# Four banks for the weight products, key products one step sooner, and a new order of the small layers

## The reference

```python
x = x + L0_xattn(layernorm(x), ctx, mask, ...)
x = x + L0_ffn(layernorm(x), ...)
x = x + L1_xattn(layernorm(x), ctx, Wq, bq, Wk, bk)
x = x + L1_ffn(layernorm(x), qweight, ...)
```

## Time and profile before

| | |
|---|---|
| median of 3 runs | 986.61 us (985.14 to 986.87) |
| the profiled execution's own time | 985.75 us |
| its span | 983.9 us |
| TensorE busy | 954.6 us, 97% of the span |
| VectorE busy | 603.1 us, 61% |
| ScalarE busy | 395.0 us, 40% |
| GpSimd busy | 470.3 us, 48% |

### The profile page before, as it was taken

The page is one execution under the profiler, slowest core; times in us unless marked ns, Lnnn a source line. Parts: engine busy times, 40 slices in busy tenths (PEclk is TensorE's granted clock), DMA queues, the critical chain, the costliest instruction groups (busy, mean ns, idle before and its releaser), DMA issues.

```text
span 983.9 us, 16715 instructions
## 1 busy us (share of the span) xinstructions
PE 954.6 (97%) x5645; PEld 835.4 (85%) x5645; DVE 603.1 (61%) x1123; ACT 395.0 (40%) x1101; POOL 470.3 (48%) x528
## 2 busy tenths in 40 slices
PE   8999999999999999999999999999999997998995
PEld 7888888888898888888888888888888886776774
DVE  5674773656566566666565656565656577274874
ACT  5655443343434343433333333334343432324553
POOL 2450735464545545555555464555554511022577
PEclk9999999999999999999999999999999999899999
DMA  9233536747474656565555656464747442111001
GB/s 335 88 95 125 171 137 210 261 157 276 156 273 161 257 176 238 190 220 190 217 200 209 219 191 241 168 257 162 256 170 261 151 150 87 52 66 33 1 34 54
DMA packets 58185, 169.60 MB, mean 172 GB/s; under 512 B 5767, under 2 KB 7947, under 8 KB 57884
## 3 DMA queue, kind: packets, MB, share of 16 engines
q1 hardware_dynamic: 58140, 169.01, 48.5%
HBM read 158.51 MB, written 10.49 MB: 172 GB/s over the span
## 4 chain that ended last, share of the span: by engine, by line
PE 91%; DVE 4%; issue 2%; ACT 1%; POOL 1%; DMA 1%; SPq 0%; POOLq 0%; ACTq 0%; DVEq 0%
PE ps_q L325 6%; PE ps_q L326 6%; PE ps_q L327 6%; PE ps_v L325 6%; PE ps_v L327 6%; PE ps_v L326 6%; PE ps_o L325 6%; PE ps_o L327 6%; PE ps_o L326 6%; PE ps_t L1775 6%; PE ps_k L325 6%; PE ps_k L327 6%; PE ps_k L326 6%; PE ps_s L1748 6%; PE ps_t L1765 3%
## 5 line engine op out<-in xcount | busy, mean ns | idle before, releaser
L1203 DVE TENSOR_TENSOR acc<-ps_o,acc 128x512 f32<-128x512 f32 x128 | 87.9, 686 | 153.3 <-PE ps_o L327 153.3
L652 ACT ACTIVATE scores<-scores,neg_max 128x128 f32<-128x128 f32 x256 | 99.9, 391 | 196.3 <-DVE neg_max L1284 196.3
L325 PE MATMUL ps_v<-wv_hi,ct_hi 128*128 128x256 f32 x504 | 143.1, 284 | 1.8 <-DVE vv L1157 1.5
L327 PE MATMUL ps_v<-wv_hi,ct_lo 128*128 128x256 f32 x504 | 142.6, 283 | 0.0
L326 PE MATMUL ps_v<-wv_lo,ct_hi 128*128 128x256 f32 x504 | 142.6, 283 | 0.0
L955 POOL TENSOR_TENSOR wq_lo<-raw_q,wq_hi 128x256 fp32r<-128x256 f32 x65 | 48.2, 742 | 158.6 <-ACT wq_hi L519 158.6
L325 PE MATMUL ps_o<-wo_hi,att_hi 128*128 128x512 f32 x256 | 105.5, 412 | 0.9 <-DVE att_lo L1191 0.9
L658 ACT COPY probs_t<-ps_t 128x512 f32<-128x512 f32 x64 | 37.6, 587 | 168.1 <-PE ps_t L1765 168.1
L325 PEld LDWEIGHTS ps_v<-wv_hi,ct_hi 128*128 128x128 f32 x504 | 96.4, 191 | 6.6 <-issue 2.5
L327 PE MATMUL ps_o<-wo_hi,att_lo 128*128 128x512 f32 x256 | 100.4, 392 | 0.0
L326 PE MATMUL ps_o<-wo_lo,att_hi 128*128 128x512 f32 x256 | 100.2, 391 | 0.0
(11 more groups left out here) (335 smaller groups left out, 2396.9 us busy)
## 6 DMA issues: line engine op xcount, KB each, us to landing
ring_hi<-scratch_x_t SPq DMA_DIRECT2D x39, 512.0 KB, 4.0
ring_lo<-scratch_x_t SPq DMA_DIRECT2D x39, 512.0 KB, 5.0
ring_hi<-scratch_c_t SPq DMA_DIRECT2D x39, 512.0 KB, 4.2
ring_lo<-scratch_c_t SPq DMA_DIRECT2D x39, 512.0 KB, 5.3
raw_v<-in_w_v SPq DMA_DIRECT2D x16, 512.0 KB, 5.7
raw_o<-in_w_o SPq DMA_DIRECT2D x16, 512.0 KB, 3.3
raw_q<-in_w_q SPq DMA_DIRECT2D x15, 512.0 KB, 5.9
raw_k<-in_w_k SPq DMA_DIRECT2D x15, 512.0 KB, 5.6
```

The costliest lines, as they stand in the source:

```text
L325: pe.matmul(dst, hi_l, hi_r, start=first, stop=False)
L327: return pe.matmul(dst, lo_l, hi_r, start=False, stop=last)
L652: e = act.activation(probs[n][:, m, :], scores[n][:, m, :], ACT.Exp, bias=neg_max[:, n, m:m + 1], accum_out=row_sum[:, n, m:m + 1])
L1203: dve.tensor_tensor(acc[:, b, :], ps_o[:], acc[:, b, :], ALU.add).then_inc(o_added, 1)
```

## The change

- **Banks.** `m_banks` gives the four weight products a bank each (`ps_q`, `ps_k`, `ps_q2`, `ps_k2`); the wait on `mm_out` is gone. `product_m(1)` and `product_m(2)` stand ahead of the matrix-vector block, with transpose and values of step 62; `product_m(3)` stands behind it. Scores of step 63 and the first half of output 62 go ahead of `spread_kb`, and `product_g(0)` goes ahead of `lora_b`.
- **Key products.** `plain_k(s + 3)` stands in step `s` in place of `plain_k(s + 2)`, from step 1 on, and ScalarE's `k_evac` with it; the one at the end of step 8 goes.
- **Evacuations.** VectorE empties the value banks for steps 62 and 63 at the end of steps 60 and 61; `attention_rest(62)` moves ahead of the copy of the matrix-vector result, `mm_rest(3)` ahead of the low-rank results.
- **Context products.** One in each of the stages 0 to 3, with one quarter of the unpacking, which moves behind `b_finish` on VectorE and to the end of the stage on ScalarE.
- **Order in the stages.** `a_rest` goes ahead of the statistics of layer 2's output; from stage 8 on, `b_finish` and its statistics go ahead of `c_scale`, and GpSimd adds the shift after `inv_std(2)`. The attention of batch 7 goes to `ps_q`. `shift_rows` is made in stage 4. `c_shift_sb` has two buffers. The shift of the last tile is one VectorE operation in stage 11, in the queue ahead of `c_rest(7)`.

```diff
@@ TensorE, steps 0 to 8
             def plain_k(t, c, bank=ps_k):
                 pe.wait_ge(wk_lo_s, 2 * (t // 4) + t % 2 + 1)
-                pe.wait_ge(k_out, min(t, 4 * PLAIN - 2))
+                pe.wait_ge(k_out, t)
...
             output(0, 0, 0, (0,))
+            plain_k(4, 4)
             step_transpose(1, 1)
...
-                plain_k(s + 2, (s + 2) % LOOP_STEPS)
+                plain_k(s + 3, (s + 3) % LOOP_STEPS)
...
             plain_q(s + 3, 3, ps_q2)
-            plain_k(s + 3, 3, ps_k2)
@@ TensorE, from layer 1 to layer 3
+        m_banks = (ps_q, ps_k, ps_q2, ps_k2)
...
-                wait_from(pe, mm_out, m - 1)
...
             output(s - 1, 5, None, (0,))
             product_m(0)
             output(s - 1, 5, None, (1,))
+            product_m(1)
+            step_transpose(s, 6)
+            product_m(2)
+            step_values(s, 6)
...
-            product_m(1)
+            product_m(3)
...
+            s = STEPS - 1
+            step_scores(s, 7)
+            output(s - 1, 6, None, (0,))
             spread_kb()
-            step_transpose(s, 6)
-            product_m(2)
-            step_values(s, 6)
...
             last.then_inc(lr_mm, 1)
-            product_m(3)
-            s = STEPS - 1
-            step_scores(s, 7)
-            output(s - 1, 6, None, (0,))
+            product_g(0)
...
-            product_g(0)
             output(s - 1, 6, None, (1,))
@@ ScalarE and VectorE, from layer 1 to layer 3
             exponentials(STEPS - 2, 0)
-            mm_high(0)
-            mm_high(1)
+            pt_evac(STEPS - 2)
+            attention_high(STEPS - 2)
+            for m in range(NC):
+                mm_high(m)
             act.wait_ge(kb_mm, 1)
             act.copy(kb_row[:], ps_v[:]).then_inc(kb_s, 1)
-            pt_evac(STEPS - 2)
-            mm_high(2)
-            attention_high(STEPS - 2)
...
-            mm_high(3)
...
-                v_evac(s + 1, ((c + 1) // 2) % 2, (c + 1) % 2)
+                if not (last and c == 5):
+                    v_evac(s + 1, ((c + 1) // 2) % 2, (c + 1) % 2)
...
+                if last and c > 3:
+                    v_evac(s + 2, 1, c % 2)
...
             softmax_front(STEPS - 2, 0)
-            v_evac(STEPS - 1, 1, 1)
...
             weighted_rows(0, wq1_raw, 1)
+            attention_rest(STEPS - 2)
             dve.wait_ge(vec_mm, 1)
...
             mm_rest(2)
-            attention_rest(STEPS - 2)
+            mm_rest(3)
...
-            mm_rest(3)
             step_drain(STEPS - 1, 7)
@@ the stages, TensorE
-                wait_from(pe, b_add, b)
-                pe.matmul(ps_o[:], b_probs_t[:], ctx_sb[:, b, :], start=True, stop=True).then_inc(at_mm, 1)
+                if b < BATCH - 1:
+                    wait_from(pe, b_add, b)
+                else:
+                    pe.wait_ge(a_add, BATCH)
+                pe.matmul((ps_o, ps_q)[b // (BATCH - 1)][:], b_probs_t[:], ctx_sb[:, b, :], start=True,
+                          stop=True).then_inc(at_mm, 1)
...
-                if w < 2:
-                    product_g(4 + 2 * w)
+                if w < 4:
+                    product_g(4 + w)
...
-                if w < 2:
-                    product_g(5 + 2 * w)
@@ the stages, ScalarE
-                wait_from(act, c_rest_s, b)
-                act.mul(c_shift_sb[:], shift_rows[:], x_sum[:, b:b + 1]).then_inc(c_shift, 1)
+                wait_from(act, c_rest_s, b - 1)
+                act.mul(c_shift_sb[b % 2][:], shift_rows[:], x_sum[:, b:b + 1]).then_inc(c_shift, 1)
...
-                if w < 2:
-                    code(2 * w)
...
-                if w < 2:
-                    code(2 * w + 1)
                 if a < BATCH:
                     stage_a_zt(a)
+                if w < 4:
+                    code(w)
@@ the stages, GpSimd
-                if c >= 0:
-                    pool.wait_ge(c_shift, c + 1)
...
+                if w < BATCH and 0 <= att:
+                    shift_in(c)
                 if 0 <= att < BATCH:
                     inv_std(2, att)
+                if w >= BATCH:
+                    shift_in(c)
@@ the stages, VectorE
+                if has_a:
+                    a_rest(a)
                 if 0 <= a - 1 < BATCH:
                     statistics(1, a - 1, a_add, a)
-                if has_a:
-                    a_rest(a)
-                if w < 2:
-                    g_evac(4 + 2 * w)
-                    unpack_code(2 * w)
+                if w < 4:
+                    g_evac(4 + w)
+                if has_att and w >= BATCH:
+                    b_finish(att)
+                    statistics(2, att, b_add, att + 1)
                 if has_c:
                     c_scale(c)
...
-                if has_att:
+                if has_att and w < BATCH:
                     b_finish(att)
                     statistics(2, att, b_add, att + 1)
-                if att == 0:
+                if w < 4:
+                    unpack_code(w)
+                if w == 4:
                     dve.wait_ge(rows_in, 48)
...
+                if w == BATCH + 3:
+                    last = BATCH - 1
+                    dve.wait_ge(c_bias, BATCH)
+                    dve.wait_ge(n_xn[2], BATCH)
+                    dve.scalar_tensor_tensor(f_scr[last % 2][:], shift_rows[:], x_sum[:, last:BATCH], f_scr[last % 2][:],
+                                             ALU.mult, ALU.add).then_inc(shift_s, 1)
             dve.wait_ge(c_scaled, BATCH)
-            dve.wait_ge(c_rest_s, BATCH)
+            dve.wait_ge(shift_s, 2)
```

34 lines of the change are left out of this document (17 added, 17 removed).

## The result

| | before | with the change |
|---|---|---|
| median | 986.87 us (5 runs, 985.14 to 989.29) | 980.50 us (5 runs, 978.06 to 981.15) |
| ratio | | 0.9937, 95% interval 0.9923 to 0.9951 |
| profiled execution | 985.75 us, span 983.9 | 981.03 us, span 979.2 |

The change makes the kernel 6.4 us faster. The forecast was 976.3 us with a range up to 980.5, and the median came out at that upper end: direction right, size 10.3 us forecast and 6.4 measured. The largest part of what is missing went in the last stages, where I had a loss of 1.1 us.

What follows compares the result with a forecast made beforehand. TensorE was taken as the bound: busy throughout the loop, with waits and a lowered clock outside it. Terms -1.0 - 8.3 - 2.1 + 1.1 = -10.3 from 985.75, plus 0.86, gave 976.3 us; range 974.0 to 980.5.

Steps and rivals of the forecast that it cites:

- Key products, -1.0: Steps 1 to 8: a key product covers TensorE's 1.41 us softmax wait, less a new 0.4 us wait; lead -1.0 us.
- Transition, -8.3 with the value evacuations: Layer 1 to layer 3: weight products, transpose and values fill the 4.8 us wait before the matrix-vector products; lead -8.3 us.
- the wait of 1.3 us for the softmax: Transition: TensorE waits 1.3 us before output 62's second half, until VectorE's add behind the last softmax frees ps_o.
- both forecast waits: Transition: new TensorE waits of about 0.7 us for kb_row and 1.3 us for ps_o.
- the fall: Rival: the granted clock falls in the transition, one or two products at the lower level; 978 to 981 us, chance 0.16.
- Context products, -2.1: Layer 2's first stages, 876.8 to 924: context products over four stages end z_stack and most a_lo waits; lead -2.1 us.
- The rival that the stages gain nothing: The normalisation chain bounds each of the first four stages; 978.4 us, up to 980.5, chance 0.13.
- the new waits: Stages: TensorE waits 1.0, then some 0.4 us for the normalised tile, 0.2 to 0.35 for z_stack, 0.6 for b_full.
- The last stages, +1.1: From stage 8: VectorE's shift waits for GpSimd's bias and c_rest queues behind it; 1.1 us of lead lost.
- No charge for the small waits: New short TensorE waits charged nothing for the clock, which stayed at 1.00 through 3.1 us of such pauses before.
- Slower than before: Rival: the clock drops in interleaved stages 1 to 4, 2.4 us per product, up to 993 us; chance 0.03.

Runs made afterwards that it cites:

- keys_back: The change with only the key products of steps 4 to 11 back in their old places; 980.46 us, ratio 0.9948.
- Pool_after_shift: Rest_first with GpSimd's shift of tile 6 held until VectorE's shift of tile 7 is done; 975.95 us (one execution).
- kb_early: Rest_first with the key bias broadcast moved ahead of the first half of output 62; 974.69 us, ratio 0.9884.
- spread_back: The change with context products 4 to 7 back in stages 0 and 1, two in each, unpacking and casts as before; 982.46 us, ratio 0.9965.
- Rest_first: The change with VectorE's shift of the last tile moved behind c_rest of that tile; 975.26 us, ratio 0.9897.
- trans_back: The change with the part from layer 1 to layer 3 undone (weight product banks, engine orders, value evacuations); 986.49 us, ratio 1.0002.
- kb_soft: kb_early, plus VectorE and ScalarE doing the last softmax before the low-rank results; 974.25 us, ratio 0.9882.

## Why the prediction was right or wrong

- **Key products, -1.0:** right in sign and mechanism. 1.5 us by the stretch, with a wait of 0.27 us for wk_lo where 0.4 was forecast. The ratios of keys_back give 1.1 but don't settle it. That the lead late in the loop was 1.1 too is chance: the slower loop took the difference.
- **Transition, -8.3 with the value evacuations:** sign and mechanism right, size 1.8 us off: 6.5 by the stretch. The failed sentence is that small products and context product take 2.85 and 2.73 us. They took 4.25 and 4.86, 3.5 us more; the matrix-vector products were 0.6 us quicker, and the slow clock hid the wait of 1.3 us for the softmax, as I had allowed. Pool_after_shift, with the clock up, has both forecast waits at their sizes, and its transition is 8.3 us shorter than before (93.84 - 85.57): the walk was right but for the clock. I had given the fall a chance of 0.16. It came in eight of the nine profiles with the low-rank products in one piece ahead of the context product (kb_early not counted, where it came later, behind the wait for VectorE). The row to read was rows 7: before, the fall had come behind the same small products, and my reason against it, that the 4.8 us pause is gone, said nothing on them. (What ran slow there, from 851.08, was the fourth weight product, not the first context product as the rows and the prediction call it; that one came at 859.79 and ran at full clock.) This is the line that opens it, before:

```profile
851.01 0.50 PE L325 MATMUL ps_k<-wq_hi,wk_hi 128*128 128x512 f32 x1
```

- **Context products, -2.1:** right: 7.6 to 9.5 us of lead, 1.9. The rival that the stages gain nothing is refuted, by the stretch (63.84 and 61.95) and by spread_back's time. Of the new waits, that for the normalised tile came as walked; those for z_stack did not come, and b_full's were shorter.
- **The last stages, +1.1:** wrong, 4.8, and this is the step of the forecast that failed most. It was seen (c_rest queued behind the shift that waits for GpSimd's bias) and under-priced in three terms. GpSimd's bias ended 1.0 us later than I had it (969.17 plus 9.45 us of lead = 978.6 on the old scale, against 977.6): GpSimd began on the statistics that I counted from 0.4 us later (958.47, 967.9 on the old scale, against 967.53), and its six whole-tile operations start 1.4 us apart, where I had 1.25. The shift took 1.73 us, not 0.7: I priced it by VectorE operations that read PSUM or ran beside an idle GpSimd. The profile before has the dearer price as well, on an operation with all operands in SBUF; 64 of them take 691 ns at the least and 2856 at the most:

```profile
L1293 DVE TENSOR_TENSOR scores<-scores,row_fac x64: 691/692/2856, 41.9 to 860.4; 128x512 f32<-128x512 f32 x64
```

And scaling and product behind c_lo took 1.6 us more than I had, the last product 3.70 us in place of 2.2. 1.0 + 1.0 + 1.6 = 3.6, the difference. Rest_first shows that 3.9 of the 4.8 hung on one place in VectorE's queue.
- **No charge for the small waits, against the rule of the Trainium skill** (TensorE: Matmul & The Clock Gate, "A second HAM failure mode: psum-queue depth-cycling"): right for the stages of the change, where the window from 876.8 to 916.4 has waits in every stage and a granted clock of 1.00, as in twelve of the thirteen versions run; in spread_back it fell there once, behind a wait of 1.76 us. In the change the falls came in two other places: behind a piece of small products, and at a single wait of 4.7 us ahead of the last product.
- **Slower than before:** did not come, but the margin is all the transition's: without it the rest came out at 1.0002 (trans_back).

## What to carry to other kernels

When an operation moves to another engine, look first at what stands behind it in that engine's queue and when its own inputs come: here one position cost 3.9 us of a lead of 9.5. Price a whole-tile VectorE operation on SBUF by a row in which GpSimd is at work. Compare profiles over a stretch and not at a position, since the unchanged loop alone differs by 1.2 us between executions. And look for pieces of small matmuls ahead of wide ones: spread between the wide ones they cost 0.3 us, and in the one profile of that order the slow stretch was gone, when removing the waits around them (kb_soft) had not done it.
